# A Perceiver layer on one core: queries' RMS factor moved into the softmax's scale, rotary part first, smaller first transfers, a split store

## What is computed

```python
def rms_norm(x, w, eps=EPS):
    var = jnp.mean(x * x, axis=-1, keepdims=True)
    return w * (x * jax.lax.rsqrt(var + eps))
cq = rms_norm(hidden_states @ w_qa.T, q_a_ln_w)           # 384 wide
q = (cq @ w_qb.T).reshape(b, s, H, DQ).transpose(0, 2, 1, 3)
q_nope, q_pe = q[..., :DN], q[..., DN:]                    # 128 and 64 wide, 16 heads
q_pe = q_pe * cos + rotate_half(q_pe) * sin
ckv = hidden_states @ w_kva.T                              # 128 latents and 64 rotary
ckv_l = rms_norm(ckv[..., :KVLR], kv_a_ln_w)
kv = (ckv_l @ w_kvb.T).reshape(b, s, H, DN + DV).transpose(0, 2, 1, 3)
scores = jnp.einsum('bhqd,bhkd->bhqk', q_full, k_full) * DQ ** -0.5
attn = jax.nn.softmax(jnp.where(causal, -jnp.inf, scores), axis=-1)
```

## Time and profile before

| | us |
|---|---|
| median of 3 runs | 715.83 |
| lowest and highest run | 715.8 and 716.37 |
| the profiled execution, device time | 716.18 |
| its span, first to last instruction | 714.3 |
| PE busy | 700.1 |

### The profile page before, as it was taken

The page is one execution under the profiler, slowest core; times in us unless marked ns, Lnnn a source line. Parts: engine busy times, 40 slices in busy tenths (PEclk is TensorE's granted clock), DMA queues, the critical chain, the costliest instruction groups (busy, mean ns, idle before and its releaser), DMA issues.

```text
span 714.3 us, 20505 instructions
## 1 busy us (share of the span) xinstructions
PE 700.1 (98%) x8725; PEld 455.7 (64%) x8725; DVE 610.9 (86%) x950; ACT 439.0 (61%) x610; POOL 11.6 (2%) x36
## 2 busy tenths in 40 slices
PE   8999999999999998998999999999999999999998
PEld 3555555555555554546777767777777777777775
DVE  5679999999999999877889977888888888888885
ACT  4778888787878887735677753444444344444442
POOL 3000000000000000010000000000000000000000
PEclk9999999999999999999999999999999999999999
DMA  8570101010110000032334403678777776777770
GB/s 322 175 276 3 62 3 62 3 61 10 54 25 39 3 3 3 3 128 98 112 121 155 161 1 105 224 215 250 220 246 222 242 239 227 245 225 243 230 238 32
DMA packets 29880, 94.44 MB, mean 132 GB/s; under 512 B 5824, under 2 KB 15088, under 8 KB 28400
## 3 DMA queue, kind: packets, MB, share of 16 engines
q1 hardware_dynamic: 28944, 92.31, 39.2%
q10 hardware_dynamic: 864, 1.07, 0.4%
HBM read 92.76 MB, written 0.57 MB: 131 GB/s over the span
## 4 chain that ended last, share of the span: by engine, by line
PE 91%; ACT 3%; DVE 3%; DMA 1%; issue 1%; POOL 0%; ACTq 0%; DVEq 0%
PE pS L1268 40%; PE pP L1268 30%; PE pO L1268 12%; PE pD L1268 8%; ACT arena L577 2%; DMA arena<-in_ctxT 1%; PE pO L1657 1%; ACT arena L618 0%; DVE xn L1183 0%; DVE xn L807 0%; POOL arena L439 0%; DVE bn L800 0%; DVE arena L1075 0%; DVE arena L790 0%; DVE arena L780 0%
## 5 line engine op out<-in xcount | busy, mean ns | idle before, releaser
L1268 PE MATMUL pS<-arena 128*128 128x256 f16 (+3 forms) x2185 | 253.5, 272 | 1.4 <-ACT arena L708 0.5
L1268 PEld LDWEIGHTS pS<-arena 128*128 128x128 f16 (+1 forms) x2185 | 213.4, 101 | 45.5 <-ACT arena L625 1.9
L1268 PE MATMUL pP<-arena 128*32 128x512 f16 (+1 forms) x2996 | 239.8, 380 | 0.2 <-ACT arena L471 0.2
L1268 PEld LDWEIGHTS pP<-arena 128*32 128x32 f16 (+1 forms) x2996 | 109.0, 97 | 102.0 <-issue 2.2
L531 ACT ACTIVATE arena<-pS,mblk 128x1024 f32<-128x1024 f32 x112 | 128.9, 1206 | 4.9 <-PE pS L1268 4.7
L1094 DVE SCALAR_TENSOR_TENSOR arena<-arena 128x1536 f16<-128x1536 f32 x72 | 126.1, 1752 | 0.8 <-ACT arena L687 0.8
L729 ACT ACTIVATE arena<-pS 128x256 f32<-128x256 f32 x72 | 27.6, 383 | 154.2 <-PE pS L1268 154.2
L1268 PE MATMUL pO<-arena 128*32 128x256 f32 (+6 forms) x1370 | 106.6, 357 | 1.7 <-DVE arena L1080 1.4
L687 ACT ACTIVATE arena<-arena 128x1536 f16<-128x1536 f32 x72 | 106.3, 1477 | 1.0 <-PE pP L1268 1.0
L936 DVE TENSOR_SCALAR arena<-arena 128x1024 f32<-128x1024 f32 x112 | 73.1, 689 | 7.0 <-ACT arena L531 7.0
L1268 PE MATMUL pD<-arena 128*128 128x512 f16 x288 | 77.8, 379 | 0.0
(11 more groups left out here) (260 smaller groups left out, 527.9 us busy)
## 6 DMA issues: line engine op xcount, KB each, us to landing
arena<-in_units SPq DMA_DIRECT2D x72, 768.0 KB, 5.0
arena<-w_scratch SPq DMA_DIRECT2D x136, 64.0 KB, 2.7
arena<-in_ctxT SPq DMA_DIRECT2D x7, 1024.0 KB, 5.3
mw_in<-in_mla_in SPq DMA_DIRECT2D x8, 832.0 KB, 6.8
mw_out<-in_mla_out SPq DMA_DIRECT2D x8, 512.0 KB, 3.8
wlatT<-in_wlatT SPq DMA_DIRECT2D x1, 1280.0 KB, 10.7
arena<-in_wkT SPq DMA_DIRECT2D x4, 256.0 KB, 5.4
arena<-in_ctxT ACTq DMA_DIRECT2D x4, 256.0 KB, 6.4
```

The source lines that it names most:

```text
L1268: return pe.matmul(o, lhsT, rhs, start=start, stop=stop, **kw)
```

## The change

- The queries' latents are no longer multiplied by their RMS factor. DVE multiplies them by the norm's weight alone (`q_latents`), which needs no sum. Only the keys' factor is on the way to the transposition (`kv_latents`), and POOL's power for it is of one column.
- The squares of the keys' latents are taken before those of the queries, and the queries' second half of squares is taken later. The queries' factor is made later by POOL for both halves at once. `q_scales` makes of it `qsc` and `nqsc`. All exponentials of the pairs take `qsc` as a per-partition scale instead of an immediate number, and the maxima are multiplied by `nqsc` (a tensor by tensor operation instead of tensor by number).
- PE transposes the second half's latents before any `first_part`, and then computes the rotary part first, then keys, then queries. The reading engines follow that order.
- At the start the first weights come in two halves of 256 columns, chunk 0 of the context in 96 partitions on ACT's queue and 32 on SP's. ACT splits the first weights in two. PE runs 7 matmuls on zeros instead of 10.
- The last store is halved: SP stores 64 partitions, ACT the other 64.

```diff
@@ sync: the first transfers, the last store
-                sp.dma_start(wk32[:, c], a["wkT"][:, c]).then_inc(first_in[c], 16)
+                if c:
+                    sp.dma_start(wk32[:, c], a["wkT"][:, c]).then_inc(first_in[c], 16)
+                    continue
+                sp.dma_start(wk32[:, 0, 0:256], a["wkT"][:, 0, 0:256]).then_inc(first_in[0], 16)
+                sp.dma_start(cbuf[96:128, 0, 0], a["ctxT"][0][96:128, 0]).then_inc(first_in[0], 16)
+                sp.dma_start(wk32[:, 0, 256:512], a["wkT"][:, 0, 256:512]).then_inc(s["wk_rest_in"], 16)
...
-            sp.dma_start(out[:, 1, :], work[:, 1, :]).then_inc(s["out_stored"], 16)
+            sp.dma_start(out[0:64, 1, :], work[0:64, 1, :]).then_inc(s["out_stored"], 16)
@@ gpsimd
-                pool.tensor_tensor(lrs[:, t], ssq[:, t], nhalf[:, :], ALU.pow).then_inc(s["lrstd_ready"], 1)
+                pool.tensor_tensor(lrs[:, t, 1:2], ssq[:, t, 1:2], nhalf[:, 0:1], ALU.pow).then_inc(s["lrstd_ready"], 1)
+            pool.wait_ge(s["qvar_ready"], 1)
+            pool.tensor_tensor(lrs[:, :, 0], ssq[:, :, 0], nhalf[:, :], ALU.pow).then_inc(s["qrs_ready"], 1)
@@ scalar
-                act.dma_start(cbuf[:, 0, c], a["ctxT"][0][:, c]).then_inc(first_in[c], 16)
+                rows = slice(0, 96 if c == 0 else 128)
+                act.dma_start(cbuf[rows, 0, c], a["ctxT"][0][rows, c]).then_inc(first_in[c], 16)
...
-                act.activation(wk16[:, 0, c], wk32[:, c], ACT.Copy, scale=SW).then_inc(s["wk_hi"], 1)
+                if c == 0:
+                    act.activation(wk16[:, 0, 0, 0:256], wk32[:, 0, 0:256], ACT.Copy, scale=SW).then_inc(s["wk_hi"], 1)
+                    act.wait_ge(s["wk_rest_in"], 16)
+                    act.activation(wk16[:, 0, 0, 256:512], wk32[:, 0, 256:512], ACT.Copy, scale=SW).then_inc(s["wk_hi"], 1)
...
+            kv_squares(0)
+            q_squares(0)
+            kv_squares(1)
...
-                                              scale=S_SCALE, accum_out=sm[:, t, j:j + 1])
+                                              scale=qsc[:, t, 0:1], accum_out=sm[:, t, j:j + 1])
...
-            mla_evac_k(0, 0, 1)
+            act.wait_ge(s["latn_ready"], 3)
+            q_squares(1)
+            mla_evac_k(0, 0, 2)
+            rope_hi(0, 0)
             mla_evac_q(0, 0, 3)
-            rope_hi(0, 0)
...
+            act.wait_ge(s["out1_ready"], 1)
+            act.dma_start(out[64:128, 1, :], work[64:128, 1, :]).then_inc(s["out_stored"], 16)
@@ vector
+            def q_latents(t):
+                dve.wait_ge(s["qsq_ready" if t == 0 else "kvsq_ready"], t + 1)
+                dve.tensor_tensor(latc[:, t, 0:QLR], lat_raw[t][:, 0:QLR], lnw_b[:, 0:QLR], ALU.mult)                   .then_inc(s["latn_ready"], 1)
...
+            def q_scales():
+                dve.wait_ge(s["qrs_ready"], 1)
+                for o, f in ((qsc, S_SCALE), (nqsc, -S_SCALE)):
+                    last = dve.tensor_scalar(o, lrs[:, :, 0:1].broadcast_to([128, TT, 2]), f, None, ALU.mult)
+                link(last)
...
-                dve.tensor_scalar(nm, mx, -S_SCALE, None, ALU.mult).then_inc(s["negmax"], 1)
+                dve.tensor_tensor(nm, mx, nqsc, ALU.mult).then_inc(s["negmax"], 1)
...
-            rope_mul(0, 0, 2)
+            rope_mul(0, 0, 1)
             lo_k(0, 0, 1)
+            rope_lo(0, 0)
             lo_q(0, 0, 2)
-            rope_lo(0, 0)
+            q_scales()
@@ tensor
-            for _ in range(10):
+            for _ in range(7):
...
-            first_part(0, False, 2)
-            first_part(0, True, 2)
             turn_latents(1)
-            for n in (1, 0):
+            for low in (False, True):
+                for n in (1, 0, 2):
+                    first_part(0, low, n)
+            for n in (1, 0, 2):
                 for low in (False, True):
-                    first_part(0, low, n)
-            for low in (False, True):
-                for n in (0, 1, 2):
                     first_part(1, low, n)
```

More of the change, by code:

```diff
@@ L172, in build @@
         epsv = take(TT)
+        qsc, nqsc = (take(2 * TT).rearrange("p (t j) -> p t j", t=TT) for _ in range(2))
         xsum = take(TT)
@@ L469, in _ @@
             for c in range(HC):
-                act.wait_ge(first_in[c], 32)
-                act.activation(wk16[:, 0, c], wk32[:, c], ACT.Copy, scale=SW).then_inc(s["wk_hi"], 1)
+                act.wait_ge(first_in[c], 32 if c else 48)
+                if c == 0:
+                    act.activation(wk16[:, 0, 0, 0:256], wk32[:, 0, 0:256], ACT.Copy, scale=SW).then_inc(s["wk_hi"], 1)
+                    act.wait_ge(s["wk_rest_in"], 16)
+                    act.activation(wk16[:, 0, 0, 256:512], wk32[:, 0, 256:512], ACT.Copy, scale=SW).then_inc(s["wk_hi"], 1)
+                else:
+                    act.activation(wk16[:, 0, c], wk32[:, c], ACT.Copy, scale=SW).then_inc(s["wk_hi"], 1)
                 if c == 1:
@@ L606, in _, with kv_squares, q_squares @@
                                accum_out=xsq[:, t:t + 1]).then_inc(s["xsq_ready"], 1)
-            for t in range(TT):
+            def kv_squares(t):
                 act.wait_ge(s["lat_mm"], t + 1)
-                act.activation(latc[:, t, 0:QLR], lat_raw[t][:, 0:QLR], ACT.Square, scale=float(QLR) ** -0.5 / (SX * SW),
-                               accum_out=ssq[:, t, 0:1])
-                act.activation(latc[:, t, QLR:LAT], lat_raw[t][:, QLR:LAT], ACT.Square, scale=float(KVLR) ** -0.5 / (SX * SW),
-                               accum_out=ssq[:, t, 1:2]).then_inc(s["ssq_ready"], 1)
+                act.activation(lat_sq[:, t, QLR:LAT], lat_raw[t][:, QLR:LAT], ACT.Square, scale=float(KVLR) ** -0.5 / (SX * SW),
+                               accum_out=ssq[:, t, 1:2]).then_inc(s["kvsq_ready"], 1)
+            def q_squares(t):
+                act.activation(lat_sq[:, t, 0:QLR], lat_raw[t][:, 0:QLR], ACT.Square, scale=float(QLR) ** -0.5 / (SX * SW),
+                               accum_out=ssq[:, t, 0:1]).then_inc(s["qsq_ready"], 1)
+            kv_squares(0)
+            q_squares(0)
+            kv_squares(1)
             def mla_exps(m):
@@ L1063, in _ @@
             add_eps(0)
-            norm_latents(0)
+            q_latents(0)
+            kv_latents(0)
             rotate_keys(1)
             add_eps(1)
+            q_latents(1)
+            kv_latents(1)
             lo_latents(0)
-            norm_latents(1)
             dve.wait_ge(s["kpe_hi"], 1)
@@ L1071, in _ @@
             lo_latents(1)
+            dve.wait_ge(s["qsq_ready"], TT)
+            dve.tensor_tensor(ssq[:, :, 0], ssq[:, :, 0], epsv[:, :], ALU.add).then_inc(s["qvar_ready"], 1)
             def rope_mul(m, p, at=None):
@@ L1338, in _ @@
                     for n in range(HC):
+                        if c == 0 and k == 0 and n == 2:
+                            pe.wait_ge(s["wk_hi"], 2)
                         unit_part(unit_bank(0, n), 0, n, c, (k,))
```

25 lines of the change are left out of this document (12 added, 13 removed).

## The result

The changed kernel takes **720.1 us** (median of 6 runs, 718.55 to 721.67), the kernel before 715.82 (6 runs beside them, 715.69 to 716.37): ratio 1.0058, 95% interval 1.0041 to 1.0074. It is slower by 4.3 us, and the forecast of 715.4 was wrong, its range too. One run of the kernel before and one of an experiment (halves by rows) took 1210 and 1213 us at a mean granted clock of 0.56 and are left out of all medians and ratios.

The account below looks back on a forecast made before the run. PE was taken as the bound, holding 91% of the chain. Start -0.45, latents -1.0, pairs +1.0 and end 0 sum to -0.45: profiled 716.18 becomes 715.7, median forecast 715.4, range 714.0 to 717.0.

Parts of the forecast that it names:

- The start: First weights, context and tokens: chunk 2 of the context lands sooner, 0.45 us gained, between -0.1 and 0.65.
- (1): Chunk 0's gate needs 384 KB instead of 512; PE begins at about 4.9 instead of 5.65, hidden behind the norm.
- (4): SP issues two more transfers first; queues are backed up, so a byte's place matters and not the issue.
- The third rival: At the start nothing is gained: chunk 2 no sooner, or eight matmuls at 0.43 instead of 0.22; 715.9, chance 0.2.
- The latents: Second layer, before the first scores: keys' latents ready sooner, scores 1.0 us earlier, between 0.7 and 1.36.
- The last rival: Second layer: the new order of latents gives nothing, squares or queries' copy in the way; 716.4, chance 0.08.
- The pairs: Head pairs: a per-partition scale costs 0.09 per exponential; 0.36 + 0.48 + 0.16 seen by PE, 1.0 us lost.
- The first rival: Head pairs: the scale operand is free, they cost nothing and the gains stay; 714.4, chance 0.17.
- the second: Head pairs: all cover goes because ACT's copies and the next scores come later too; 717.3, chance 0.12.
- The end: Last store halved over two queues: same 512 KB through 16 full engines, 0 taken, from -0.2 to 0.2.

Follow-up runs that it names:

- halves by rows: Kernel before with the first weights' transfer issued as two of 64 rows each on SyncE's queue, conversions waiting for both; 718.90 us, ratio 1.0029.
- the start alone: Kernel before with only the change's split first weights, 96/32 context piece over two queues and seven zero matmuls; 719.29 us, ratio 1.0044.
- the order alone: Kernel before with only the first pair's work reordered to rotary, keys, queries on PE, ACT and DVE; RMS factor and scale unchanged; 715.97 us against 716.02.
- the kernel without the operand: Kernel with only new latents and softmax scale, but exponentials and negated maximum use the constant scale, RMS factor not applied; 715.70 us against 716.02.
- 496 and 16 columns: Kernel before with the first weights' transfer issued as two on SyncE's queue, of 496 and of 16 columns; 719.06 us, ratio 1.0040.
- the split 96/32: Kernel before with the first context piece split 96/32 rows over two queues, the 32 second on SyncE's, weights whole; 718.43 us, ratio 1.0034.
- transfer of 127 rows: Kernel before with the first weights' transfer issued as two on SyncE's queue, of 127 rows and of one row; 731.24 us, ratio 1.0211.

## Why the prediction was wrong, step by step

**The step that failed** is in "The start", points (1) and (4): PE "begins at about 4.9", "hidden behind the norm", and "a byte's place in them matters and not the issue". It priced the first half of the weights and never asked when the second half, which the third matmul needs, would land, nor when chunk 1's would with three transfers ahead instead of one. By its own rate they would have been early enough: SyncE's queue moved 1.34 MB in 7.9 us, so 320 and 576 KB take 1.9 and 3.4 us from 1.6 on, and with the 1.9 from there to the landing that chunk 0's 256 KB show (4.97), both would be in by 5.4 and 6.9. They were in at 8.4 and 10.5, and by 10.5 the queue had moved 1.42 MB: the bytes were moved, but not in the order in which a place in the queue would have them. In the kernel before all these transfers are of 256 KB, one to a chunk, so no row there could tell a rate from anything that goes by the transfer; the text took the rate. It forecast -0.45; the start alone gave +3.4.

**The clock.** The third rival named the mechanism (real matmuls at 0.43) and gave it 1.7 us "where it has 0.75 + 0.83 to spare". It put the idle time before the first matmul, 0.5 us; the idle time was behind the second, 3.19 in the profiled execution. What the seven zeros left uncovered cost 0.7 by the medians, not clear of their spread. Its price of 715.9 needed the cover of 1.6 us that the waits had already eaten.

**The latents**: -1.0 forecast, -0.97 in the trace. The sum over POOL, DVE and the 66 matmuls was right, and what is late next was named (DVE's three low parts). The last rival (order gives nothing) fell in the full kernel, though the order alone does give next to nothing.

**The pairs**: +1.0 forecast, +1.2 in the trace and about 1.3 by the kernel without the operand. 0.36 for pair 0 and 0.16 for the last (0.14) were right, pairs 4 and 5 untouched as said; pairs 1 to 3 lost 0.23 each and not 0.16, so the cover there was 0.13 and not 0.2. Mechanism right, one term mis-sized. The first rival (operand free) and the second (all cover goes) both fell.

**The end**: 0 forecast with 0.2 either side, +0.9 in the trace. The full share of the 16 engines in the earlier trace rows was right as far as it goes, but it prices the bytes and not the two ends of a transfer. The split is 0.6 of it, from whichever queue. The other part, an instruction block fetched beside the store, stood in no row that was read (its packet of before is at 716, behind the span's end); it can't be read from the diff, and it is 1.0 where the store is whole.

Had the start been left alone and the store too, the terms that were right would have summed to +0.2 and the block would have made it +1.1. The edit that was meant as the safest, smaller pieces first, carried the loss.

## What to carry to other kernels

Where transfers queue behind each other at the start, count them: one more ahead of the weights that PE needs put these 2 to 4 us back here, even one of 8 KB, and when a gate is split, price the landing of the last piece and of what is queued behind, not of the first. A per-partition operand in an activation costs 0.09 us each time, and only what stands between two engines that wait on it is seen. When a kernel is slower by a microsecond with no cause in its chain, look at what is fetched beside the last store, and shift a program's length by a few waits to see whether it goes away.

## What the runs showed that was not expected

- Landings do not go by the bytes ahead in the queue: with one transfer ahead chunk 1's weights were used at 6.31 to 6.53, with two at 8.37 to 10.28, with three at 9.15 to 10.52, for 256 to 320 KB ahead, and by 10.2 us the queue with 496 and 16 columns had moved 1.29 MB where 0.52 lay up to their end.
- A split start scatters: 3.1 us between six runs of the changed kernel (1.9 for the start alone, 2.6 for the split 96/32), where the kernel before stays within 1.1. The half of the weights landed between 4.1 and 6.7 us after its issue.
- SyncE's issue itself took up to 2.37 us for the sixth or seventh transfer of a split start, 0.4 to 0.64 for all of them before.
- A transfer of 127 rows held the kernel up by 15 us.
- One packet of 8 KB of instructions beside the last store went with 1.0 us more until the store had landed, and 24 waits at the head of VectorE's program, 700 us earlier, removed both.
- Two halves of a store of 256 KB end 0.6 us later than the whole, from one queue as from two.
